# Last sparse unit of a four-stage transformer kernel: low parts and ranking moved to VectorE in two halves of 256 tokens

## The reference, cut to what matters

```
x = _layernorm(x + _L0_attn_ref(x))
x = _layernorm(x + _L0_ffn_ref(x, ...))
x = _layernorm(x + _L1_attn_ref(x, ...))
x = _layernorm(x + _L1_ffn_ref(x, w_gate, w_up, w_down))

def _L1_ffn_ref(x, w_gate, w_up, w_down):
    h = silu(x @ w_gate) * (x @ w_up)          # 256 -> 1024
    # of each 4 neighbours of h the 2 of largest magnitude are kept, the others become 0
    g = h.reshape(B, S, I // 4, 4)
    _, idx = top_k(abs(g), 2)
    h_sparse = (g * mask(idx)).reshape(B, S, I)
    return h_sparse @ w_down                   # 1024 -> 256
```

## Time and profile before

| what | value |
|---|---|
| median of three runs | 1228.03 us (1227.83 to 1228.88) |
| the profiled execution's own time | 1228.34 us |
| its span in the trace | 1226.5 us |
| TensorE matmuls | busy 1189.2 us, 97% of the span, 7168 |
| VectorE | busy 826.0 us, 67%, 1550 instructions |
| ScalarE | busy 615.1 us, 50% |
| GpSimd | busy 420.4 us, 34% |
| mean granted TensorE clock | 0.991 |

### The profile page before, as it was taken

The page is one execution under the profiler, slowest core; times in us unless marked ns, Lnnn a source line. Parts: engine busy times, 40 slices in busy tenths (PEclk is TensorE's granted clock), DMA queues, the critical chain, the costliest instruction groups (busy, mean ns, idle before and its releaser), DMA issues.

```text
span 1226.5 us, 20808 instructions
## 1 busy us (share of the span) xinstructions
PE 1189.2 (97%) x7168; PEld 1019.8 (83%) x7168; DVE 826.0 (67%) x1550; ACT 615.1 (50%) x1242; POOL 420.4 (34%) x561
## 2 busy tenths in 40 slices
PE   6899999999999999999999999999999999999996
PEld 6788888888888888888877788887877788888886
DVE  5787635445353544534469888888875999898998
ACT  4444323233332323333458998989885554444441
POOL 1203100000000000000047888888884434444434
PEclk8999999999999999999999999999999999999998
DMA  5222100101010010100001011110111000111101
GB/s 206 88 68 91 35 1 1 35 1 35 1 35 1 2 32 0 52 0 18 1 13 35 28 53 52 51 30 21 51 52 35 27 16 20 34 34 34 34 18 35
DMA packets 31113, 42.21 MB, mean 34 GB/s; under 512 B 2576, under 2 KB 23056, under 8 KB 30928
## 3 DMA queue, kind: packets, MB, share of 16 engines
q1 hardware_dynamic: 31056, 41.45, 10.5%
HBM read 27.94 MB, written 12.58 MB: 33 GB/s over the span
## 4 chain that ended last, share of the span: by engine, by line
PE 87%; DVE 7%; ACT 3%; issue 2%; POOL 0%; DMA 0%; POOLq 0%; DVEq 0%; ACTq 0%; SPq 0%; PEldq 0%
PE bank L48 26%; PE bank L50 24%; PE bank L49 24%; PE bank L1996 2%; PE bank L1977 2%; PE bank L1987 1%; PE bank L1959 1%; PE bank L1923 1%; DVE beats L1567 1%; PE bank L1967 1%; DVE dab L1584 1%; PE bank L1878 1%; PE bank L1730 1%; PE bank L1879 1%; DVE dh L1551 1%
## 5 line engine op out<-in xcount | busy, mean ns | idle before, releaser
L1274 DVE TENSOR_TENSOR hb<-gl,bank 128x512 f32<-128x512 f32 x128 | 87.9, 687 | 202.3 <-PE bank L50 197.3
L793 ACT ACTIVATE hh<-hb 128x512 fp32r<-128x512 f32 x128 | 80.9, 632 | 185.1 <-DVE hb L1274 185.1
L838 ACT ACTIVATE gl<-bank 128x512 f32<-128x512 f32 x128 | 76.7, 599 | 184.9 <-PE bank L50 184.9
L1237 DVE TENSOR_TENSOR hl<-hb,hh 128x512 fp32r<-128x512 f32 x128 | 93.7, 732 | 78.9 <-ACT hh L793 78.9
L771 POOL TENSOR_TENSOR dhl<-dab,dhh 128x512 fp32r<-128x512 f32 x63 | 95.4, 1536 | 126.7 <-ACT dhh L793 126.6
L580 POOL TENSOR_TENSOR veb<-mvb,eps 128x4 f32<-128x4 f32 x8 | 1.6, 201 | 317.5 <-DVE mvb L1254 317.5
L48 PE MATMUL bank<-xt_l,w_h 128*128 128x512 f32 x256 | 102.7, 401 | 1.0 <-DVE dh L1551 0.5
L48 PE MATMUL bank<-at_l,w_hi_a 128*128 128x512 f32 x256 | 102.8, 402 | 0.6 <-PE bank L50 0.3
L50 PE MATMUL bank<-at_h,w_hi_b 128*128 128x512 f32 x256 | 101.4, 396 | 0.0
L50 PE MATMUL bank<-at_h,w_hi_a 128*128 128x512 f32 x256 | 101.3, 396 | 0.0
L48 PE MATMUL bank<-at_l,w_hi_b 128*128 128x512 f32 x256 | 101.3, 396 | 0.0
(11 more groups left out here) (256 smaller groups left out, 3565.1 us busy)
## 6 DMA issues: line engine op xcount, KB each, us to landing
xg<-x_scratch SPq DMA_DIRECT2D x16, 512.0 KB, 3.9
xg<-in_xt SPq DMA_DIRECT2D x8, 512.0 KB, 4.8
x_scratch<-rows_out SPq DMA_DIRECT2D x8, 512.0 KB, 3.1
x_scratch<-rows_out SPq DMA_DIRECT2D x16, 256.0 KB, 2.2
xall<-in_x SPq DMA_DIRECT2D x7, 512.0 KB, 8.9
out<-rows_out SPq DMA_DIRECT2D x7, 512.0 KB, 3.2
wq<-in_codes SPq DMA_DIRECT2D x12, 256.0 KB, 2.7
sc<-in_scales SPq DMA_DIRECT2D x12, 256.0 KB, 3.0
```

Of the source, the lines that this page charges most:

```text
L793: return act.activation(dst, src, ACT.Copy)
L838: act.activation(gl[:, n % 2], ps_gate[n % 2][:], ACT.Gelu_apprx_tanh).then_inc(s_gelu, 1)
L1237: return dve.tensor_tensor(dst, src, hi.bitcast(F32), ALU.subtract)
L1274: dve.tensor_tensor(hb[:, n % 2], gl[:, n % 2], ps_up[n % 2][:], ALU.mult).then_inc(s_h, 1)
```

## The change

For the last unit alone, VectorE works on two halves of 256 tokens, one after the other. For each half it makes the three comparisons, six rank instructions, four keeps and four low parts, all on half-width tiles. ScalarE copies the high parts in eight half-width copies, four for each half. GpSimd makes no low part of this unit any more. TensorE makes the down products of the first two token blocks for all r, then those of the last two blocks, and each r waits for one low part of its half. The down sum of the first half is signalled after the first 24 matmuls, and no longer after 42 of the 48.

```
@@ GpSimd
-            unit(MB * GROUPS - 1, 1, 1)
             inv_std(GROUPS - 2, mv, ve, rstd, d_ln, d_lnr)
@@ ScalarE
             act.wait_ge(d_down, GROUPS - 1)
-            for r in range(RANK):
-                kept_hi(MB * GROUPS - 1, 1, r)
+            for half in range(2):
+                part = slice(half * H, half * H + H)
+                for r in range(RANK):
+                    act.wait_ge(d_sel, RANK * (MB * GROUPS - 1) + RANK * half + r + 1)
+                    copy(dhh[:, 1, r, part], dab[:, 1, r, part]).then_inc(d_hi, 1)
@@ VectorE
-            for r in range(RANK):
-                if r == RANK - 1:
-                    dve.wait_ge(d_hi, RANK * (MB * GROUPS - 1) + 1)
-                    lo_part(dhl[:, 1, 0], dab[:, 1, 0], dhh[:, 1, 0]).then_inc(d_lo_last, 1)
-                sparsify(MB * GROUPS - 1, 1, r)
+            def sparsify_last(half):
+                m = MB * GROUPS - 1
+                part = slice(half * H, half * H + H)
+                if half == 0:
+                    dve.wait_ge(d_abs, RANK * (m + 1))
+                for one, to, count in PAIRS:
+                    dve.tensor_tensor(beats[:, to:to + count, part],
+                                      dab[:, 1, one:one + 1, part].broadcast_to([P, count, H]),
+                                      dab[:, 1, one + 1:, part], ALU.is_ge).then_inc(d_cmp, 1)
+                dve.wait_ge(d_cmp, len(PAIRS) * (m + half + 1))
+                dve.tensor_tensor(rank[:, 0:2, part], beats[:, 1:4:2, part], beats[:, 2:5:2, part], ALU.add).then_inc(d_add, 1)
...
+                dve.wait_ge(d_add, RANK_STEPS * (m + half) + 1)
+                dve.tensor_tensor(rank[:, 0, part], rank[:, 0, part], beats[:, 0, part], ALU.add).then_inc(d_add, 1)
...
+                for r in range(RANK):
+                    dve.wait_ge(d_add, RANK_STEPS * (m + half) + 3 + r)
+                    value, op = KEEP[r]
+                    dve.scalar_tensor_tensor(dab[:, 1, r, part], rank[:, r, part], value, dh[:, 1, r, part], op,
+                                             ALU.mult).then_inc(d_sel, 1)
+                for r in range(RANK):
+                    dve.wait_ge(d_hi, RANK * (m + half) + r + 1)
+                    lo_part(dhl[:, 1, r, part], dab[:, 1, r, part], dhh[:, 1, r, part]).then_inc(d_lo_last, 1)
+
+            for half in range(2):
+                sparsify_last(half)
             add_x3(GROUPS - 2)
@@ TensorE
-            for m in range(MB * GROUPS - 2, MB * GROUPS):
+            for r in range(RANK):
+                down1(MB * GROUPS - 2, 0, r, GROUPS - 1)
+            for half in range(2):
                 for r in range(RANK):
-                    down1(m, m % MB, r, GROUPS - 1)
+                    pe.wait_ge(d_lo_last, RANK * half + r + 1)
+                    at = 2 * KT * MLP1 + (RANK + r) * H
+                    for t in range(2 * half, 2 * half + 2):
+                        mm = exact3(pe, last_tile[t], dhh[:, 1, r, t * P:(t + 1) * P], dhl[:, 1, r, t * P:(t + 1) * P],
+                                    w1h[:, at:at + H], w1l[:, at:at + H], start=False, stop=r == RANK - 1,
+                                    skip_group_check=True)
+                mm.then_inc(d_down, 1)
```

More of the change, by code:

```diff
@@ L766, in _, with unit @@
             pool.wait_ge(c_x3, NT * GROUPS)
-            def unit(m, mb, first=0):
-                for r in range(first, RANK):
+            def unit(m, mb):
+                for r in range(RANK):
                     pool.wait_ge(d_hi, RANK * m + r + 1)
@@ L1646, in _ @@
             unit(MB * GROUPS - 1, 1, True)
-            for r in range(RANK):
-                if r == RANK - 1:
-                    dve.wait_ge(d_hi, RANK * (MB * GROUPS - 1) + 1)
-                    lo_part(dhl[:, 1, 0], dab[:, 1, 0], dhh[:, 1, 0]).then_inc(d_lo_last, 1)
-                sparsify(MB * GROUPS - 1, 1, r)
+            def sparsify_last(half):
[9 more added lines that the diff above has]
+                dve.tensor_tensor(rank[:, 0:2, part], beats[:, 1:4:2, part], beats[:, 2:5:2, part], ALU.add).then_inc(d_add, 1)
+                dve.tensor_tensor(rank[:, 2:4, part], beats[:, 1:3, part], beats[:, 3:5, part], ALU.add).then_inc(d_add, 1)
+                dve.wait_ge(d_add, RANK_STEPS * (m + half) + 1)
+                dve.tensor_tensor(rank[:, 0, part], rank[:, 0, part], beats[:, 0, part], ALU.add).then_inc(d_add, 1)
+                dve.tensor_tensor(rank[:, 1, part], rank[:, 1, part], beats[:, 0, part], ALU.subtract).then_inc(d_add, 1)
+                dve.wait_ge(d_add, RANK_STEPS * (m + half) + 2)
+                dve.tensor_tensor(rank[:, 2, part], beats[:, 5, part], rank[:, 2, part], ALU.subtract).then_inc(d_add, 1)
+                dve.tensor_tensor(rank[:, 3, part], beats[:, 5, part], rank[:, 3, part], ALU.add).then_inc(d_add, 1)
+                for r in range(RANK):
[6 more added lines that the diff above has]
+                    lo_part(dhl[:, 1, r, part], dab[:, 1, r, part], dhh[:, 1, r, part]).then_inc(d_lo_last, 1)
@@ L2108, in down1 @@
                 last = isinstance(g, int) and g == GROUPS - 1
[L2109 to L2113, removed]
+                pe.wait_ge(d_lo, RANK * m + r + 1)
                 if last and mb == 0 and r == 0:
@@ L2119, in down1 @@
                 for t in range(NT):
-                    if last and mb == MB - 1 and r == RANK - 1 and t == 2:
-                        mm.then_inc(d_down, 1)
                     mm = exact3(pe, (last_tile if last else down_tile)[t], dhh[:, mb, r, t * P:(t + 1) * P], dhl[:, mb, r, t * P:(t + 1) * P],
```

2 lines of the change are left out of this document (1 added, 1 removed).

## The result

The changed kernel takes **1230.32 us** (median of 20 runs) against 1228.32 us for the kernel before (median of 20 runs). The ratio is 1.0016, with a 95% interval from 1.0011 to 1.0022: 2.0 us slower, 1.4 to 2.7. One of the 20 executions of the changed kernel took 1651.86 us at a mean granted TensorE clock of 0.655; it is left out of the ratio and moves the median by 0.03. Forecast were 1229.7 us, within 1228.4 to 1231.2, and +0.13%, within 0.2%; all three hold for the median, though the interval of the ratio reaches 0.22%. Of the 0.6 us between forecast and median, 0.3 is the kernel before, whose median was 1228.03 us in three runs and is 1228.32 in twenty. What is left, +2.0 against the forecast +1.63, lies inside the interval.

The account below looks back on a forecast made before the run. VectorE's program in the last unit was taken to bound the end: low parts +2.06, additional starts +0.9, less 1.12 of collision and 0.16 of wait, worked out as +1.63 on 1228.03, giving 1229.7 us, range 1228.4 to 1231.2.

Parts of the forecast that it names:

- +1.63: VectorE, last unit: residual sums of group 6 start 1.63 us later, at 1214.00 against 1212.37, carried whole to the end.
- What bounds the end: Chain from 1200.92 us to the end: VectorE's instructions in order, no TensorE; down products ready 1.5 to 2.5 us early.
- at least 3 us: TensorE, end: changed down products finish between 1216.0 and 1218.3, VectorE asks at 1221.8, so pause and clock are covered.
- VectorE's piece: VectorE from last unit's first comparison to group 6's residual sums: 11.45 us before; halves of 7.03 and 6.05 us after.
- narrow ranks: VectorE, last unit: eight rank instructions of 256 bf16 elements, priced at a spacing of 0.20 us each.
- +2.35: VectorE's sum if each narrow rank cost 0.29 us, an estimate from the skill page's 150 cycles.
- the stretch of the last keeps: VectorE, last two keeps beside GpSimd's low part at 1210.02: removing the collision saves 2.41 - 1.29 = 1.12 us.
- The rivals: Four alternatives: down products set the end (5%), narrow instructions dear (12%), ScalarE paces low parts (7%), give and take even out (6%).
- narrow instruction was dear: Rival on VectorE's eight narrow ranks: at 0.33 us each the sum is +2.7 us, 1230.7 us; 12%.
- ScalarE paced nothing: Rival that ScalarE's high-part copies pace the low parts: +0.9 us more, 1230.6 us; 7%.
- the first comparison's stretch: VectorE beside GpSimd's unit 14 low part: 0.98 us stays; rival with less, down to nothing, gives +0.65, 1228.7 us; 6%.
- the second rival: Narrow instructions are dear: VectorE's eight narrow ranks at 0.33 us each, +2.7 us, 1230.7 us; 12%.

Follow-up runs that it names:

- the new order: Last group's first-half sums and statistics ahead of group 6's normalisation on VectorE: on the changed kernel ratio 1.0005, on the kernel before 0.9999.

## Why the prediction was right, point by point

- **What bounds the end.** Forecast: VectorE's program from the last comparison on, no TensorE in it. Shown by the delayed products: 2.4 us later without any effect, and by a wait of 0.23 us when they came 4.8 us later. I had written "at least 3 us" of cover; it was 4.5.
- **VectorE's piece.** Forecast +1.63, measured +1.72 in the trace. The narrow ranks, the one price without a row, are spaced 0.20 us as worked out from the rows of 512 and 1024 elements. The Trainium skill, page "VectorE: DVE Perf Modes", section "The TRN2 errata — SBUF-src ops pay a fixed extra latency per instruction", measures a fixed term of about 150 cycles; taken as a spacing it gave an estimate of 0.29 us, which the trace does not bear out. The measured +2.0 us lies halfway between my +1.63 and the +2.35 of that reading, so the time alone would not have told them apart: the spacings do. Keeps and low parts are spaced 0.33, and the first comparison lasted 1.94 us, 0.99 more than the 0.95 of its own.
- **ScalarE.** Forecast: no wait, 0.43 us a copy. Its group in the changed kernel:

```profile
L792 ACT ACTIVATE dhh<-dab 128x256 fp32r<-128x256 f32 x8 | 2.8, 413 | 9.6 <-DVE dab L1670 9.6
```

  The copies took 0.41, and the low parts followed the keeps without a pause.
- **GpSimd.** Forecast: its removal saves VectorE the stretch of the last keeps and nothing else. The keeps are at 0.33 and the wait for the inverse deviations is still 1.40 us. The same keeps in full width, with no GpSimd work beside them, are spaced 0.60.
- **The rivals.** No narrow instruction was dear, ScalarE paced nothing, the first comparison's stretch stayed. None of the four occurred.
- **Where it came near to failing.** The measured +2.0 us is 0.3 to 0.4 over what the traces show, and its interval reaches 2.7, beyond the 2.46 that I called measurable. My sum took the 1.8 us outside the span as unchanged; they grew by 0.2, and why is open. For the last 0.1 to 0.2 no step answers; the spread in the start of the last unit, 1.7 us between executions, is larger.
- **A slip in the range.** Its upper end is 1231.2, but the sum given for it, 1230.7 for the second rival plus 0.3 of spread, is 1231.0. The median lies under both.

What the change does to TensorE is what it aims at: the first half's products are done 6 us before they were (the 24th matmul starts at 1210.35, the 42nd of before at 1216.68). The time does not fall because this lies on an engine that nobody waited for, and was paid for on the one that sets the end.

## What to carry to other kernels

Before splitting work so that a second engine can start earlier, look whether anybody waits for that engine at the end of the chain, and split only the instructions whose results it needs: here the keeps and low parts, not the comparisons and ranks, a difference of 0.75 us. Price a moved instruction on the engine that takes it, on what it disturbs while it runs, and on what is queued behind it in the program of that engine. An earlier result is worth nothing until the consumer's order asks for it earlier.

## What the runs showed of the hardware that I had not expected

- Beside a GpSimd subtraction, a VectorE instruction with two SBUF inputs is not slowed evenly in these traces: one of the two hardly advances until the other is done, and it can be either. In the kernel before, the subtraction had started 0.16 us earlier and the comparison lost 0.98 us. With the halves' low parts on GpSimd, the first one started during a keep and lost: 2.80 us for 0.73, while VectorE's comparisons ran at their usual 0.95, 0.68 and 0.41. VectorE paused for 0.03 us at 1207.58, ahead of the ranks; the low part was done 0.6 us later and the rank instruction lost 0.41. From then on they took turns. The Trainium skill, page "SBUF — State Buffer", section "Who interferes with whom", has this as an exclusive lock that the first to issue holds for its whole instruction, and the traces agree for single instructions (2.74 us for the comparison beside a low part that started first). What they add is that VectorE's instructions, each started some 0.08 us before the one in front ends, kept it over three comparisons. That it passes on at a pause is my reading of one case.
- The normalisation, with one SBUF tensor and two values per partition, was stretched too, from 1.39 to 2.34 us for four, its first from 0.40 to 1.37. The statistics, and the sums out of PSUM, were not. The same section names VectorE's two-port modes as the other kind that contends; but the normalisation's spacing of 0.33 us is the same as that of the sums and keeps, so what the normalisation takes from GpSimd is left open.
- After pauses of 2.28 to 2.45 us TensorE's matmuls first ran on at a spacing of 0.12 us, and then fell to 0.21, the lower of the clock's two levels (1.2 and 2.4 GHz), for some 2 to 3.5 us: 1.2 us after work was resumed in the kernel before, 1.5 in the changed one, 1.4 in that with 16 extra matmuls. In three executions they did not fall at all: with 48 extra matmuls (pause 2.45 us), with the new order on the kernel before (2.27), and with the second half's low parts on GpSimd (2.90, longer than any of the three above). So the pause before a stretch of matmuls does not tell by itself whether they slow down, and two single executions can differ by half a microsecond of TensorE's time for that reason alone.
